# Ten tiles instead of seven fetched row by row by ScalarE, fourteen instead of nine by SyncE, in an embedding ranker on one core

## What is computed

```python
B, F, E, H = (512, 26, 64, 125000)
x0 = emb[ids].reshape(ids.shape[0], -1)
x = x0
for i in range(cross_w.shape[0]):
    s = x @ cross_w[i]
    x = x0 * s[:, None] + cross_b[i] + x
h = jax.nn.relu(x0 @ w1 + b1)      # 1664 -> 1024
h = jax.nn.relu(h @ w2 + b2)       # 1024 -> 512
h = jax.nn.relu(h @ w3 + b3)       # 512 -> 256
logit = jnp.concatenate([x, h], axis=1) @ out_w + out_b
return jax.nn.sigmoid(logit)
```

## Time and profile before

| | |
|---|---|
| median of three runs | 538.0 us (537.65 to 539.04) |
| the profiled execution, its own time | 539.25 us |
| its span in the trace | 537.4 us |
| TensorE, matmuls | 470.0 us busy, 87% |
| TensorE, weight loads | 436.3 us busy, 81% |
| GpSimd | 379.4 us busy, 71% |
| VectorE | 184.4 us busy, 34% |
| ScalarE | 104.9 us busy, 20% |
| mean granted TensorE clock | 0.994 |

### The profile page before, as it was taken

The page is one execution under the profiler, slowest core; times in us unless marked ns, Lnnn a source line. Parts: engine busy times, 40 slices in busy tenths (PEclk is TensorE's granted clock), DMA queues, the critical chain, the costliest instruction groups (busy, mean ns, idle before and its releaser), DMA issues.

```text
span 537.4 us, 11277 instructions
## 1 busy us (share of the span) xinstructions
PE 470.0 (87%) x2876; PEld 436.3 (81%) x2876; DVE 184.4 (34%) x383; ACT 104.9 (20%) x194; POOL 379.4 (71%) x407
## 2 busy tenths in 40 slices
PE   0078599999899999999898998989899897999997
PEld 0078489898898889788897988889798887988996
DVE  4464522414242331424232241423223142322325
ACT  6595511101110110111111020111111011101111
POOL 5777557577777777777777777777777777777720
PEclk9998999999999999999999999999999999999999
DMA  8992111011111111111111111111111111111100
GB/s 231 224 363 81 24 23 26 22 30 26 30 28 29 27 29 29 29 27 30 28 29 25 30 30 28 27 29 28 27 29 27 30 26 29 28 28 26 28 10 2
DMA packets 19700, 24.90 MB, mean 46 GB/s; under 512 B 9305, under 2 KB 10292, under 8 KB 19636
## 3 DMA queue, kind: packets, MB, share of 16 engines
q0 software_dynamic: 12800, 13.13, 11.9%
q1 hardware_dynamic: 4770, 10.74, 5.7%
q10 hardware_dynamic: 2066, 0.31, 0.3%
HBM read 24.41 MB, written 0.01 MB: 45 GB/s over the span
## 4 chain that ended last, share of the span: by engine, by line
PE 52%; ACTq 12%; POOL 10%; issue 9%; ACT 6%; DMA 6%; DVE 5%; POOLq 0%; DVEq 0%
PE l_bank L716 40%; ACTq L390 11%; POOL x_raw L342 10%; DMA x_raw<-in_L_rec_emb,idx 5%; PE x_bank L716 4%; PE x_bank L732 4%; PE h_bank L760 3%; ACT xT_hi L403 2%; ACT w_hi L360 2%; DVE x_raw L521 2%; ACTq L387 1%; DVE xT_lo L528 1%; PE l_bank L791 1%; ACT h_bank L370 1%; DVE h2T_lo L533 1%
## 5 line engine op out<-in xcount | busy, mean ns | idle before, releaser
L342 POOL DMA_INDIRECT x_raw<-in_L_rec_emb,idx x400 | 378.5, 946 | 134.0 <-issue 107.2
L716 PE MATMUL l_bank<-w_hi,xT_hi 128*128 128x342 f32 (+1 forms) x624 | 145.6, 333 | 10.1 <-DVE xT_lo L528 10.1
L716 PE MATMUL l_bank<-w_hi,xT_lo 128*128 128x342 f32 (+1 forms) x624 | 138.4, 322 | 0.0
L716 PE MATMUL l_bank<-w_lo,xT_hi 128*128 128x342 f32 (+1 forms) x624 | 137.9, 321 | 0.0
L716 PEld LDWEIGHTS l_bank<-w_hi,xT_hi 128*128 128x128 f32 x624 | 104.0, 191 | 15.0 <-DVE xT_lo L528 13.6
L716 PEld LDWEIGHTS l_bank<-w_hi,xT_lo 128*128 128x128 f32 x624 | 106.9, 191 | 0.0
L716 PEld LDWEIGHTS l_bank<-w_lo,xT_hi 128*128 128x128 f32 x624 | 106.8, 190 | 0.0
L528 DVE TENSOR_TENSOR xT_lo<-x_bank,xT_hi 128x512 fp32r<-128x512 f32 (+1 forms) x66 | 38.2, 578 | 168.8 <-ACT xT_hi L403 168.8
L403 ACT ACTIVATE xT_hi<-x_bank 128x512 fp32r<-128x512 f32 (+1 forms) x66 | 33.5, 507 | 261.8 <-PE x_bank L732 205.4
L732 PE MATMUL x_bank<-identity,x_raw 128*128 128x128 f32 x208 | 34.8, 280 | 44.0 <-DVE x_raw L521 26.9
L732 PEld LDWEIGHTS x_bank<-identity,x_raw 128*128 128x128 f32 x208 | 25.2, 142 | 52.6 <-issue 49.9
(11 more groups left out here) (90 smaller groups left out, 289.5 us busy)
## 6 DMA issues: line engine op xcount, KB each, us to landing
ids<-in_L_rec_emb SPq DMA_DIRECT2D x1152, 0.2 KB
ids<-in_L_rec_emb ACTq DMA_DIRECT2D x896, 0.2 KB
w_raw<-in_L_rec_w SPq DMA_DIRECT2D x18, 512.0 KB, 21.7
x_raw<-in_L_rec_emb,idx POOLq DMA_INDIRECT x400, 2.4
b_rows<-in_L_rec_b SPq DMA_DIRECT2D x1, 512.0 KB
b_rows<-in_L_rec_b SPq DMA_DIRECT2D x1, 256.0 KB
ids<-in_r_ids SPq DMA_DIRECT2D x1, 208.0 KB, 2.7
b_rows<-in_L_rec_b SPq DMA_DIRECT2D x1, 128.0 KB
```

The costliest lines, as they stand in the source:

```text
L342: pool.indirect_dma_start(out=dst, out_offset=None, in_=emb, in_offset=rows).then_inc(landed, 16)
L716: done = pe.matmul(bank[:, 0:b - a], x[:, k, :], w[:, k, a:b], start=(k == 0 and n == 0), stop=(k == last_k and n == 2))
```

## The change

SyncE fetches field 24 of all fourteen tiles from 2 to 15. ScalarE fetches field 23 instead of field 25, of ten tiles, in shares of 12, 20, 4, 28, 16 and 16 rows, 96 a step; `fetch` returns once all ten tiles are done. The addresses are laid out in four runs of evenly spaced tiles instead of three. GpSimd gathers 392 fields.

```diff
-    SP_TILES = [2, 4, 6, 8, 9, 10, 12, 14, 15]
+    SP_TILES = list(range(2, TILES))
...
-    ACT_TILES = [3, 5, 7, 9, 11, 13, 15]
-    ACT_FIELD = F - 1
+    ACT_TILES = [3, 4, 5, 7, 8, 9, 11, 12, 13, 15]
+    ACT_FIELD = F - 3
     ACT_BUFS = 2
-    ACT_SHARES = [8, 12, 4, 16, 12, 12]
+    ACT_SHARES = [12, 20, 4, 28, 16, 16]
...
+    ONE_RUNS = [(SP_FIELD, 2, 1), (ACT_FIELD, 3, 4), (ACT_FIELD, 4, 4), (ACT_FIELD, 5, 4)]
+    AT_ROWS = [(f, t) for f, a, every in ONE_RUNS for t in range(a, TILES, every)]
...
-                    sync.load(regs, at_bytes[at_row[t]:at_row[t] + 1, p:p + SP_REGS])
+                    row = AT_ROWS.index((SP_FIELD, t))
+                    sync.load(regs, at_bytes[row:row + 1, p:p + SP_REGS])
...
                 j, p = fetched[0] // P, fetched[0] % P
+                if j == len(ACT_TILES):
+                    return
+                assert p + share <= P
...
-                row = len(SP_TILES) + j
+                row = AT_ROWS.index((ACT_FIELD, ACT_TILES[j]))
...
-            for field, tiles in ((SP_FIELD, [t for t in SP_TILES if t % 2 == 0]), (SP_FIELD, [t for t in SP_TILES if t % 2]),
-                                 (ACT_FIELD, ACT_TILES)):
-                every = tiles[1] - tiles[0]
-                assert tiles == list(range(tiles[0], tiles[-1] + 1, every))
+            for field, first, every in ONE_RUNS:
+                tiles = range(first, TILES, every)
...
-            pe.wait_ge(sp_cols_ready, 3)
+            pe.wait_ge(sp_cols_ready, len(ONE_RUNS))
```

More of the change, by code:

```diff
@@ L50, in dcn_ranker_kernel @@
     assert SP_FIELD // FPK in GROUPS[-1] and SP_FIELD // FPK in LAST_GROUPS[3]
-    ACT_TILES = [3, 5, 7, 9, 11, 13, 15]
-    ACT_FIELD = F - 1
+    ACT_TILES = [3, 4, 5, 7, 8, 9, 11, 12, 13, 15]
+    ACT_FIELD = F - 3
     ACT_BUFS = 2
-    ACT_SHARES = [8, 12, 4, 16, 12, 12]
+    ACT_SHARES = [12, 20, 4, 28, 16, 16]
     assert ACT_FIELD // FPK in GROUPS[-1] and all(
-        sum(ACT_SHARES) * (t - 1) >= P * (j + 1) for j, t in enumerate(ACT_TILES)) and P % sum(ACT_SHARES) == 0
+        sum(ACT_SHARES) * (t - 1) >= P * (j + 1) for j, t in enumerate(ACT_TILES))
+    ONE_RUNS = [(SP_FIELD, 2, 1), (ACT_FIELD, 3, 4), (ACT_FIELD, 4, 4), (ACT_FIELD, 5, 4)]
+    AT_ROWS = [(f, t) for f, a, every in ONE_RUNS for t in range(a, TILES, every)]
+    assert sorted(AT_ROWS) == sorted([(SP_FIELD, t) for t in SP_TILES] + [(ACT_FIELD, t) for t in ACT_TILES])
     ROW = E * 4
@@ L150, in dcn_ranker_kernel @@
         at_bytes = sb("at_bytes", [ONE_BY_ONE, P], I32)
-        at_row = {t: i for i, t in enumerate([t for t in SP_TILES if t % 2 == 0] + [t for t in SP_TILES if t % 2])}
         VR = (2 * CROSS + 1) * K1
```

## The result

The changed kernel takes **560.6 us** (median of four runs, 559.0 to 562.0) against 538.5 us for the kernel before (also the median of four, the three runs above and one more): a ratio of 1.041, 95% interval 1.037 to 1.045. It is slower, as forecast, but by 22 us and not by 137. From h1_hi of step 1 to h1_hi of step 13 it takes 489.20 - 94.92 = 394.3 us, 32.9 us a step, where the kernel before takes 371.5 us, 31.0 a step. (Counted so, show the end of step 4 and step 5, not steps 6 and 7.)

The account below looks back on a forecast made before the run. ScalarE's queue was taken as the bound at 41.4 us a step: 68.5 + 13 x 41.4 = 606.7, plus 67.2 behind it, a span of 673.9 us, forecast 675 us, range 667 to 690.

Parts of the forecast that it names:

- the prediction's own sum: ScalarE's queue, share by share: 41.1 us plus 0.3 for slow issues, 41.4 us a step instead of 30.8.
- The price of a row on ScalarE: ScalarE's DMA issues: one more row costs 0.375 us, load included; least 0.325, most 0.40.
- The arithmetic on that price: Whole kernel: 13 steps of 41.4 us on ScalarE, plus start and tail, giving 675 us.
- the tail: Time behind x_hi of group 0 of step 14: 67.2 us, where the old kernel takes 67.6.
- the signs: Profile after: ACTq largest in the chain, steps of 41 to 42 us, issues at 235 ns, little clock loss.
- Rival (b): ScalarE's issues get cheap in long runs; below 0.265 us a row the forecast falls; 533 us at 0.257; chance 2%.
- If TensorE is never late: Condition on ScalarE's 41.4 us step: TensorE needs only 28.9 us of work, so it never answers last.
- What hangs on h2_hi: Last steps: the share of 20 delays h2_hi by 3.0 us, hidden by two chunks TensorE holds in reserve.
- GpSimd's saving: GpSimd's queue: 8 gathers fewer at 1.28 us save 10 us, mere cover beside ScalarE's 41 us step, worth nothing.
- SyncE: SyncE's fetches: 14 tiles at 32.9 us make 461 us, last rows at 501; with 41 us steps it idles at buffers.
- Rival (a): TensorE idleness before group 2 lowers the clock; two stretches a step cost 1 to 2 us more, 697 us; chance 7%.

Follow-up runs that it names:

- real addresses: Changed kernel with addresses inside the table for all of ScalarE's rows, so none of its DMAs is skipped: 687.6 us in one execution.
- the better shares: Changed kernel with ScalarE's shares 16, 16, 8, 24, 16, 16 instead of 12, 20, 4, 28, 16, 16: 533.5 us, ratio 0.991 to the kernel before.

## Why the prediction was right and wrong

That the kernel would be slower came true by luck. Put the measured 0.21 us a row into the prediction's own sum, and ScalarE's step is 41.4 - 96 x 0.165 = 25.6 us, under the 30.8 of the kernel before: by its working the change would then not be slower at all. It had two steps wrong: the price of a row, which took 137 us away, and what hangs on the place of each share, which cost the 22.

**The price of a row on ScalarE: wrong, and all the rest follows.** The step says "0.375 us a row, load included", bounded from 0.325 to 0.40. It took the 235 ns of 896 issues for a property of the engine; it was a property of their addresses. After the change 1107 of 1280 issues, 86%, are dropped and cost 90 ns, and a row, load included, costs some 0.21 us: in the step shown, 12 rows more cost 7.40 - (219.63 - 214.72) = 2.5 us. The price was bounded by rows of one kind only, and the low end of the range, 669 us, did not even use its own least of 0.325, but 0.37. The trace of before held the other kind: SyncE's issues at 73 ns with a largest of 318. Asked why one engine pays a third of the other for the same DMA, that row could have led to the bounds check and to the ids' ranges in the reference. The prediction put it down to the engine. The diff line `ACT_FIELD = F - 3` was read as a change of place.

**The arithmetic on that price: right.** With rows that move, the kernel takes 687.6 us against a forecast of 675 and a top of 690. Of the 12 us, 13 x 0.7 = 9 are the step (42.1 instead of 41.4): the share of 28 was 11.74 instead of 11.22, and h2_hi to the next x_hi took 2.86 us instead of 2.51. The other 3 us are the tail, 70.0 us behind x_hi of group 0 of step 14 instead of 67.2. ScalarE's queue has the largest part of the chain, as the signs said. The clock did not keep to them: 109 us of the main loop ran at half clock, more than 8 us a step.

**Rival (b): right that a cheap row undoes the forecast, wrong in its turning point and its mechanism.** It put the turning point at 0.265 us a row and gave it 2%. At 0.21 us a row the forecast did fall, but the kernel was still 22 us slower and not at 533 us: the rival took for granted that a step whose queue has room loses nothing. Its reason was that a longer run pays part of an issue once. There is such a part, but it is paid on top of the 235 ns: in every share of every run the first issue that moves a row takes ScalarE 459 ns or more, the others 235 to 243 ns by their median (84 shares before, 67 of the 80 after have such a row). What made the issues cheap is the address. The chance should have come from the unexplained 73 against 235, not from the least of 896 equal cases.

**"If TensorE is never late": wrong with cheap rows.** In the changed kernel TensorE answers last in three places of the step (h1_hi, x_hi of group 0, x_hi of group 1), ScalarE in two, and x_hi of group 3 goes either way. This makes the place of a row count, not only the sum: 96 rows cost 22 us in one order and gain 5 in another.

**What hangs on h2_hi: wrong.** The prediction let two chunks of reserve hide a late h2_hi. The transpose of group 1 stands behind it by way of VectorE's queue, and the 8 rows that the share ahead of it gained were part of the 22 us.

**GpSimd's saving: right in the forecast's frame, and wrong outside it.** "Cover, worth nothing" holds for the kernel with 41 us a step. With ScalarE out of the way a gather is worth 1.2 us.

**SyncE: right in size.** Forecast 461 us for fourteen tiles; the row of the changed kernel's timeline (start, us, count) shows 463, ending at 503.5. It never waited for a buffer; with steps of 42 us, under real addresses, it did, as forecast (43.1 us, 5 times).

```profile
40.52 462.99 SPq L297 DMA_DIRECT2D ids<-in_L_rec_emb  x1792
```

**Rival (a), the clock: seen, and up to a third of the loss.** Stretches of the changed kernel around one such fall, columns as in the earlier trace rows:

```profile
179.50:182.90 3.40, 1.34 (x9) 1.06 (x8) 0.95 (x2) 0.89 (x3) 2.79 (x3) 1.00 0.14 32
182.90:186.30 3.40, 3.40 (x13) 3.40 (x13) 0.10 (x1) 0.00 (x0) 2.49 (x3) 0.50 0.13 29
186.30:189.70 3.40, 3.40 (x24) 3.38 (x23) 0.42 (x1) 0.38 (x1) 2.48 (x4) 1.00 0.08 20
```

PE was busy 1.34 of 3.40 us ahead of group 2, and the next 3.4 us ran at 1.2 GHz: 13 matmuls instead of the 24 of the stretch behind. It is the pattern of the earlier trace rows. The Trainium skill (TensorE: Matmul & The Clock Gate, Part 1) states the rule, that idleness throttles the clock and activity releases it. The trace agrees. The mean clock fell from 0.994 to 0.977 here: 17 us of the main loop at half clock, none in the kernel before, and 7.5 us more for the same matmuls. With the better shares these stretches are gone, so they came with the long shares. In the kernel with real addresses the mean was 0.915. There the rival's condition, two stretches or more in a step, was met, and its price of 1 to 2 us a step was not paid in full: the step was 0.7 us over the forecast.

## What to carry to other kernels

The duration of an issue may depend on the data it is given, so before a row's price is carried to another field, tile or engine, ask which kinds of operands the row was measured on, and explain any two rows of one operation that differ by a factor. In a queue that holds both issues and arithmetic, count not only the queue's total but each stretch between two hand-offs against what the other engine needs there; moving rows between stretches was worth 27 us here, more than the change itself. Where two engines bound a step alike, lowering one shows little (0.998 for ScalarE's rows, 0.995 for GpSimd's gathers) until both are lowered (0.987).

## What the runs showed of the hardware

From issue to issue, with the register move, a dropped one costs 0.18 us on ScalarE, where one that moves costs 0.325; on SyncE it is 0.167 and 0.322. The first issue of a share that moves a row costs more: 467 ns by the median of 84 in the kernel before on ScalarE. On SyncE the first behind each load of 32 registers takes 273 ns where all rows move. Whether the load or the work ahead of it makes the first one dear was not tested. The DMA queue's packet count on the page gives the number that moved, at two packets each beside 274 of other DMAs: 2066 packets for 896 issues before, 2834 for 1280 with real addresses, and 620 for 1280 after the change, 173 of which moved.
